# Graph network on one core: 15 of 416 edge blocks gathered by TensorE, and the edge stage joined with the segment sum

## The reference, cut to what matters

```python
h = relu(layernorm(x))                              # x after the first layer
e = concat([h[src], edge_attr], axis=1)             # 212500 x 128
e = e @ W1a + b1a                                   # 212500 x 128
e = relu(batch_norm(e, g1a, be1a))                  # mean and variance over all edges
# (e @ W2a + b2a is pulled behind the sum: W2a and W1b are multiplied once)
s = segment_sum(e, dst, 12500)                      # 12500 x 128
out = x + mlp(concat([h, s @ W2a + degree * b2a]))  # second batch norm, W1b, W2b
```

## Time and profile before

| | us |
|---|---|
| median of the runs shown | 5270.26 |
| profiled execution | 5270.57, its span 5268.7 |
| stages 1 to 3, to the first gather of stage 4 | 2513.8 |
| stage 4, first gather to the last block's statistics | 2086.0 |
| hand-over to the first running sum | 22.9 |
| stage 5, first running sum to the last | 533.6 |
| rest | 112.5 |
| GpSimd busy over the span | 3541.3 (67%) |
| VectorE busy over the span | 2374.1 (45%) |
| TensorE busy over the span | 2219.0 (42%), mean granted clock 0.659 |

### The profile page before, as it was taken

How to read it: one execution, slowest core, us unless ns; L and a number is a source line. 1 busy time by engine, 2 the same in 40 slices (tenths; PEclk the granted TensorE clock), 3 DMA queues, 4 the chain that set the end, 5 groups by cost and what they waited for, 6 DMA issues and landing times. The chain is left out here.

```text
span 5268.7 us, 27205 instructions
## 1 busy us (share of the span) xinstructions
PE 2219.0 (42%) x6378; PEld 1160.9 (22%) x6378; DVE 2374.1 (45%) x2946; ACT 1143.4 (22%) x1953; POOL 3541.3 (67%) x3749
## 2 busy tenths in 40 slices
PE   2012332323323232232454455455555555467766
PEld 2001111111111111110222222222222222255545
DVE  6224454544545444457222222222222222389995
ACT  8000000000000000001222222222222222178783
POOL 6677777777777777777677777777777777611112
PEclk7556666666666666665667666666666666678897
DMA  9723333333333333332333333333333333399993
GB/s 345 241 66 80 89 82 87 89 81 89 82 88 88 82 89 81 88 84 57 96 104 105 110 99 110 105 104 110 98 110 104 105 110 98 97 384 420 414 418 100
DMA packets 351656, 710.02 MB, mean 135 GB/s; under 512 B 146453, under 2 KB 218107, under 8 KB 304804
## 3 DMA queue, kind: packets, MB, share of 16 engines
q1 hardware_dynamic: 206258, 573.15, 31.6%
q0 software_dynamic: 119072, 128.58, 11.9%
q10 hardware_dynamic: 26166, 6.56, 0.6%
HBM read 363.45 MB, written 344.48 MB: 134 GB/s over the span
## 5 line engine op out<-in xcount | busy, mean ns | idle before, releaser
L1084 POOL DMA_INDIRECT pairs<-norm_table,node_sums x1664 | 1570.2, 944 | 520.1 <-issue 504.4
L836 POOL DMA_INDIRECT hid<-send_table,node_sums x1664 | 1570.3, 944 | 507.0 <-issue 507.0
L872 PE MATMUL ps_msg<-hidden,w_quarters 128*128 128x512 f32 x832 | 616.5, 909 | 1468.6 <-ACT hidden L901 1468.6
L1188 DVE TENSOR_SCALAR hid<-ps_hid,vec 128x512 f32<-128x512 f32 x416 | 312.2, 751 | 1463.1 <-PE ps_hid L1104 1462.8
L1097 PE MATMUL ps_pairs<-ident,pairs 128*128 128x128 f32 x1664 | 398.9, 386 | 1006.0 <-DMA pairs<-norm_table,node_sums 1005.4
L1104 PE MATMUL ps_hid<-pairs_t,w1a 128*128 128x512 f32 x832 | 701.1, 941 | 0.0
L872 PEld LDWEIGHTS ps_msg<-hidden,w_quarters 128*128 128x128 f32 x832 | 238.0, 301 | 1846.9 <-ACT hidden L901 1534.4
L940 DVE STREAM_TRANSPOSE send_t<-hid 128x1024 f32<-128x1024 f32 x104 | 131.0, 1260 | 1045.2 <-DMA hid<-send_table,node_sums 1045.2
L1097 PEld LDWEIGHTS ps_pairs<-ident,pairs 128*128 128x128 f32 x1664 | 265.7, 195 | 1449.8 <-issue 1282.0
L1136 ACT COPY pairs_t<-ps_pairs 128x512 f32<-128x512 f32 x416 | 243.6, 586 | 1485.9 <-PE ps_pairs L1097 1479.8
L901 ACT ACTIVATE hidden<-joined 128x1024 f32<-128x1024 f32 x104 | 109.9, 1056 | 1969.1 <-DVE joined L944 1969.1
(11 more groups left out here) (195 smaller groups left out, 1899.2 us busy)
## 6 DMA issues: line engine op xcount, KB each, us to landing
hid_edges<-hid SPq DMA_DIRECT2D x104, 1024.0 KB
hid<-hid_edges SPq DMA_DIRECT2D x104, 1024.0 KB, 10.9
hid_edges<-rows SPq DMA_DIRECT2D x104, 1024.0 KB
recv_edges<-node_sums SPq DMA_DIRECT2D x52, 1024.0 KB
hid<-recv_edges SPq DMA_DIRECT2D x416, 128.0 KB, 3.3
recv_edges<-hid SPq DMA_DIRECT2D x416, 128.0 KB, 2.3
edge_in<-in_edge_attr_dram SPq DMA_DIRECT2D x415, 128.0 KB, 4.6
hid<-send_table,node_sums POOLq DMA_INDIRECT x1664
```

Of the source, the lines that this page charges most:

```text
L836: pool.indirect_dma_start(out=send_in[:, s, j * C:(j + 1) * C], out_offset=None, in_=send_table, in_offset=bass.IndirectOffsetOnAxis(ap=sr ...
L872: mm = nc.tensor.matmul(ps_msg[k % M][:, d, :], w2_quarters[:, b, d, :], hidden[:, s % 2, b, :], start=b == 0, stop=b == BANDS - 1)
L1084: pool.indirect_dma_start(out=pairs[:, s, j, 0:C], out_offset=None, in_=norm_table, in_offset=bass.IndirectOffsetOnAxis(ap=src_cols[:, k / ...
L1188: nc.vector.tensor_scalar(part, ps_hid[s % 2][:, :], vec[:, 0:1], None, ALU.add).then_inc(hid_made, 1)
```

## The change

Five things change, all in stages 4 and 5.

1. **Products for gathers.** From block 36 on (`FIRST`), every 24 blocks form a group, 15 groups in all, and the last block of each has no indirect DMA. Its rows come from TensorE. In blocks 8 to 35 the table in SBUF is split into three bf16 parts (high, middle, rest) by ScalarE and VectorE. For the product block VectorE makes a small one-hot of "node number modulo 128" times "tile number + 1" (`make_own`), TensorE turns it into PSUM (`turn_own`), and over the 23 other blocks of the group VectorE makes 98 one-hot tiles of 128 x 512 bf16 out of it (`make_hot`, 8 buffers), four or five per block. For each of them TensorE runs two products (`add_tiles`): 128 columns for high and middle, 64 for the rest. ScalarE copies the sums out in three pieces, and `product` adds one more product with W1a's node half stacked twice.
2. **Last to first.** Blocks are walked from 415 down to 0, so that chunks 4 to 0 come last. They stay in SBUF, in a ring of five slots, and are neither stored nor loaded.
3. **One block of code.** Stages 4 and 5 have no barrier between them. The first relu waits for `affine_made` alone; the masks are loaded by SP in front of that.
4. **Statistics in parts.** Every 51 blocks VectorE aggregates their statistics into two sets of six; the last aggregation reads 16 sets instead of 416.
5. **Smaller moves.** Edge attributes are loaded straight into `pairs`, in pieces of 256 bytes, without ScalarE's copy. The running sum works in place, in the chunk's own slot, so that a slot is loaded again only when its chunk has been turned back.

The diff, cut to its core:

```diff
+            HR = 5
+            SPLIT = 3
+            TILES = NI
+            FIRST = U + 2 * NSTEP3
+            GROUP = 24
+            NPE = 15
+            OH = 8
+            hot_of = ps_mask[1][:, BLK:BLK + BLK // 2].bitcast(BF16)
...
+            def block_of(k):
+                return NBLK - 1 - k
+            def slot_of(c):
+                return c if c < HR else c % 2
+            def by_products(k):
+                g, at = group_of(k)
+                return 0 <= g < NPE and at == GROUP - 1
+            def tiles_of(k):
+                g, at = group_of(k)
+                if not 0 <= g < NPE or at == GROUP - 1:
+                    return range(0)
+                return range(TILES * at // (GROUP - 1), TILES * (at + 1) // (GROUP - 1))
...
-                def load(r, s):
-                    k = r * U + s
-                    at_least(sp, edge_copied, k - U + 1)
+                def load_pairs(r, s):
+                    k = r * U + s
+                    at_least(sp, turned, k - U + 1)
...
+                        sp.dma_start(pairs[:, s, :, C:2 * C], attr_v[block_of(k)]).then_inc(loaded[s], 16)
+                def store_hid(r, s):
+                    k = r * U + s
+                    c = chunk_of(k)
+                    if k % PER != PER - 1 or c < HR:
+                        return
...
+                sp.wait_ge(hot_used, TILES * NPE)
+                sp.dma_start(masks, same_sum.rearrange("(p c) -> p c", c=CO)).then_inc(masks_in, 16)
+                def load_hid(k, _):
+                    if k < HR:
+                        return
+                    at_least(sp, back_turned, 2 * (k - HR + 1))
+                    at_least(sp, sum_done, 2 * (k - HR + 1) + 1)
+                    sp.dma_start(hid[:, k % HR, :], hid_v[:, k, :]).then_inc(hid_back[k % HR], 16)
...
                 def gather(r, s):
                     k = r * U + s
-                    at_least_apart(pool, turned, k - U + 1, pool_passed)
+                    b = block_of(k)
+                    if by_products(k):
+                        return
+                    at_least(pool, turned, k - U + 1)
...
+                    own = by_products(k)
+                    if own:
+                        nc.tensor.matmul(ps_hid[s % 2], w_twice[:, :], sums_hm, start=True, stop=False)
+                    nc.tensor.matmul(ps_hid[s % 2], w1a[:, :], pairs_t[:, s % 2, :], start=not own, stop=True).then_inc(multiplied, 1)
...
+                def add_tiles(r, s):
+                    k = r * U + s
+                    g, _ = group_of(k)
+                    n = hot_count(k)
+                    for t in tiles_of(k):
+                        if t == 0:
+                            at_least(pe, last_made, NSTEP3)
+                            at_least(pe, sums_taken, 2 * g)
+                        at_least(pe, hot_made, n + 1)
+                        first, last = t == 0, t == TILES - 1
+                        nc.tensor.matmul(acc_hm, table_hm[:, t, :, :].rearrange("p h c -> p (h c)"), one_hot[:, n % OH, :], start=first, stop=last)
+                        mm = nc.tensor.matmul(acc_lo, table_lo[:, t, :], one_hot[:, n % OH, :], start=first, stop=last)
+                        mm.then_inc(hot_used, 1)
+                        n += 1
...
-                pipeline(pe, NBLK, U, [(0, turn), (1, product), (NODE_EVERY, product_node), (0, turn_node)])
+                pipeline(pe, NBLK, U, [(0, turn), (1, product), (2, product_node), (0, turn_node), (0, add_tiles), (0, turn_own)])
...
+                def make_hot(r, s):
+                    k = r * U + s
+                    g, _ = group_of(k)
+                    n = hot_count(k)
+                    for t in tiles_of(k):
+                        if t == 0:
+                            at_least(dve, own_turned, g + 1)
+                        at_least(dve, hot_used, n - OH + 1)
+                        nc.vector.tensor_scalar(one_hot[:, n % OH, :], hot_of, float(t + 1), None, ALU.is_equal).then_inc(hot_made, 1)
+                        n += 1
...
-                pipeline(dve, NBLK, U, [(0, finish)])
+                pipeline(dve, NBLK, U, [(0, split), (0, make_hot), (0, make_own), (3, finish), (3, aggregate)])
                 dve.wait_ge(stats_made, NBLK)
-                affine_of_norm(Chain(dve, sem("affine4")), root_ready, root_made, stats[:, :, :].rearrange("p k q -> p (k q)"),
+                affine_of_norm(Chain(dve, sem("affine4")), root_ready, root_made, parts[:, :, :].rearrange("p k q -> p (k q)"),
...
-        end_phase()
...
-        with ExitStack() as s5:
-            U = 12
-            R = 3
-            HR = 4
...
-                        at_least(act, loaded[s % HR], 16 * (r * (U // HR) + s // HR + 1))
+                    if h == 0 and k >= HR:
+                        at_least(act, hid_back[k % HR], 16 * (k // HR))
...
-                pipeline(sp, CHUNKS, U, [(5, store), (0, load), (8, confirm)])
+                pipeline(sp, CHUNKS, 1, [(0, load_hid), (4, store_rows), (7, confirm)])
```

More of the change, by code:

```diff
@@ new lines, in gnn_kernel @@
+            w_in, turned, copied, multiplied, hid_made, stats_made, root_ready, root_made, affine_made = (
+                sem(n + "4") for n in ("w_in", "turned", "copied", "multiplied", "hid_made", "stats_made", "root_ready", "root_made", "affine_made"))
+            hid_back = [sem(f"hid_back{i}") for i in range(HR)]
+            rows_out = [sem(f"rows_out{i}") for i in range(R)]
+            numbered, own_made, own_turned, hot_used, hot_made, sums_taken, high_made, rest_made, mid_made, last_made = (
+                sem(n + "4") for n in ("numbered", "own_made", "own_turned", "hot_used", "hot_made", "sums_taken", "high_made", "rest_made",
+                                       "mid_made", "last_made"))
@@ L1086, in gather @@
                                                 ).then_inc(gathered[s], 16)
                 pipeline(pool, NBLK, U, [(0, gather)])
+                pool.wait_ge(node_taken, NI_PAD)
+                pool.wait_ge(hot_used, TILES * NPE)
+                pool.wait_ge(chunks_out, HR)
+                for i in range(NI):
+                    needed = pool.value_load(chunks_needed[0:1, i:i + 1], min_val=1, max_val=CHUNKS)
+                    pool.wait_ge(chunks_out, needed)
+                    pool.sem_inc(pool_passed, 1)
+                    pool.indirect_dma_start(out=sum_in[:, i, :], out_offset=None, in_=sum_edges,
+                                            in_offset=bass.IndirectOffsetOnAxis(ap=end_idx[:, i:i + 1], axis=0)).then_inc(sums_got, 16)
@@ L1093, in turn @@
                     k = r * U + s
-                    at_least(pe, edge_copied, k + 1)
-                    at_least(pe, gathered[s], 16 * J * (r + 1))
+                    at_least(pe, loaded[s], 16 * (r + 1))
+                    at_least(pe, gathered[s], 16 * J * gathers_of(k))
                     for j in range(J):
@@ new lines, in _, with spread @@
+                pe.wait_ge(hid_made, NBLK)
+                pe.wait_ge(node_copied, NI_PAD)
+                pe.wait_ge(node_made, NI)
+                pe.wait_ge(sums_taken, 2 * NPE)
+                def spread(k, h):
+                    at_least(pe, sum_done, 2 * k - 1 + h)
+                    one_row = row_of[0:NCO, k:k + 1].broadcast_to([NCO, P])
+                    for a in range(0, HALF, BLK):
+                        mm = nc.tensor.matmul(ps_mask[h][:, a:a + BLK], one_row, masks[:, h * HALF + a:h * HALF + a + BLK], start=True, stop=True)
+                    mm.then_inc(mask_spread, 1)
@@ new lines, in turn_back @@
+                def turn_back(k, h):
+                    if h == 0:
+                        at_least(pe, sum_done, 2 * (k + 1))
+                    at_least(pe, rows_made, 2 * k + h - 1)
+                    for j in range(JS // 2):
+                        mm = nc.tensor.transpose(ps_back[h][:, j * P:(j + 1) * P], hid[:, k % HR, h * (JS // 2) + j::JS], ident[:, :])
+                    mm.then_inc(back_turned, 1)
+                pe.wait_ge(begun, 2)
+                pe.wait_ge(masks_in, 16)
@@ new lines, in copy_rows @@
+                def copy_rows(k, h):
+                    at_least(act, back_turned, 2 * k + h + 1)
+                    if h == 0:
+                        at_least(act, rows_out[k % R], 16 * (k // R))
+                    nc.scalar.copy(rows[:, k % R, h * HALF:(h + 1) * HALF], ps_back[h][:, :]).then_inc(rows_made, 1)
+                pipeline(act, CHUNKS, 1, [(0, lambda k, _: relu(k, 0)), (2, lambda k, _: copy_rows(k, 0)),
+                                          (0, lambda k, _: relu(k, 1)), (2, lambda k, _: copy_rows(k, 1))])
@@ L1326, in gnn_kernel @@
+                    part = hid[:, k % HR, h * HALF:(h + 1) * HALF]
+                    nc.vector.tensor_tensor_scan(part, ps_mask[h][:, :], part, before, ALU.mult, ALU.add).then_inc(sum_done, 1)
+                pipeline(dve, CHUNKS, 1, [(0, lambda k, _: running_sum(k, 0)), (0, lambda k, _: running_sum(k, 1))])
```

373 lines of the change are left out of this document (219 added, 154 removed).

## The result

The changed kernel takes 5174.95 us (median of four runs, 5173.9 to 5176.39). The kernel before, beside it, took 5270.03 (5268.15 to 5272.83): a ratio of 0.982, with a 95% interval of 0.9805 to 0.9834. 5166 was forecast, with a range of 5140 to 5230. The profiled spans are 5268.7 and 5173.8, 94.9 us apart.

| stretch | before | after | difference | forecast |
|---|---|---|---|---|
| to the first gather of stage 4 | 2513.7 | 2512.9 | -0.8 | 0 |
| first to last gather | 2076.1 | 2001.4 | -74.7 | -74.9 |
| last gather to last statistics | 10.0 | 8.2 | -1.8 | 0 |
| last statistics to first running sum | 22.87 | 3.38 | -19.5 | -19.6 |
| first running sum to the last one's end | 533.6 | 533.7 | +0.1 | -10.2 |

A forecast was written before the change was run, and what follows sets the result against it. GpSimd's issuing of gathers was taken to bound stage 4, and DMA transfers stage 5. Savings of 74.9 (gathers), 19.6 (hand-over) and 10.2 (stage 5), together 104.7, from 5270.57 gave 5166 us, range 5140 to 5230.

The forecast's parts named there:

- GpSimd sets the pace, 74.9 us: Stage 4: GpSimd, issuing gathers, is the engine waited for; 15 blocks x 4 gathers x 1.248 us leave the time.
- The others hold the new pace: Stage 4: per group VectorE (67 to 111 us) and TensorE (if its clock rises) fit into GpSimd's 114.9 us.
- the rivals' mechanism: Stage 4: groups outlast GpSimd's 114.9 us, through seams and long one-hots (5191 us, chance 0.17) or slow clock (5503, 0.10).
- The clock rises when TensorE has products between its waits: Stage 4 groups: TensorE waits less than before, reaching the mean clock of 0.71 to 0.89 it needs, against 0.65.
- The rule that was weighed as a rival: Stage 4: each wait slows TensorE, clock stays 0.65, groups 10 to 35 us longer, 5316 to 5690 us; chance 0.10.
- The hand-over, 19.6 us: Last statistics to first running sum: 3.3 us in place of 22.87, with short aggregation and no load in front.
- Stage 5, 10.2 us: Running-sum stage: five chunks needn't be loaded, so 523.4 us in place of 533.6; bounds of the saving 0 and 24.
- 7.4 + 525 - 8.6 = 523.4: Stage 5 length: transfers start 7.4 us after first running sum, take 525 at 418 GB/s; last sum ends 8.6 before last transfer.
- The other 24 us belong to the loads: Stage 5 before the change: 208 running sums need 510 us of 534; the remainder was put down to waiting for loads.
- The rival of 510 us: Stage 5 runs at VectorE's pace, 510 us in place of 523, if loads are freed; total 5152 us, chance 0.07.

## Why the prediction was right, and where it was not

**GpSimd sets the pace, 74.9 us: right.** 74.7 in the trace, 75.0 by taking the products out alone, and 9.05 more for two further blocks.

**The others hold the new pace: right, with less to spare on TensorE than on VectorE.** The one-hot was taken at 0.49 us and is 0.418; VectorE has 72 us per group, near the lower end of its 67 to 111. The Trainium skill, "VectorE: DVE Perf Modes", section "Why PSUM operands drop a tier", has two 16-bit elements per cycle from PSUM at most. The trace agrees, with 0.418 us against the f32 row's 0.751 and the 0.39 estimated from the page. TensorE went the other way. A pair of products was bounded by 0.40 and 0.61 us at the fast level, and starts lie 0.66 apart. A group came to 104.3 us of TensorE, the upper end of 83 to 104, at a clock of 0.96 where 0.71 to 0.89 was asked for. The high clock paid for the long pairs. The groups of 16 show what stood behind this step: where TensorE falls late, the time does come out of the total, and the rivals' mechanism is real (shown there by more work per group, not by a slower clock or longer one-hots). In the groups of 24 it was some 10 us away (114.9 - 104.3).

**The clock rises when TensorE has products between its waits: right.** 0.64 in the blocks of stage 4 ahead of the groups, 0.96 in them. Only 126 waits for gathers are left of 381. The rule that was weighed as a rival is that of the Trainium skill, "TensorE: Matmul & The Clock Gate", section "HAM oscillation — how this bites in real kernels", which tells of a kernel where every wait for a tile put the array back to its slow level. Here it is seen at single waits, as in the block above with its 1.09, but not at each: of the 83 waits for a gather in the groups, 29 are followed by transposes that take over 0.9 us, and the others, up to 3.12 us long, are not. The earlier trace rows had a block at the fast level behind a wait already (1.49 us), which the prediction read as agreeing with that rule.

**The hand-over, 19.6 us: right.** 19.5, by the steps named: 3.38 us where 3.3 was worked out. Of its parts, the chunks that stay were taken back by a run (8.1 us); the aggregation's 11.42 to 0.59 and the missing barrier are read from the traces alone.

**Stage 5, 10.2 us: wrong, it gave nothing.** The step that failed is "7.4 + 525 - 8.6 = 523.4". Each of its parts was off, and the prediction's 7.4 left out a step: SyncE asks for a chunk behind the store of the chunk that stood in the slot:

```profile
4535.89 0.34 SPq L1195 DMA_DIRECT2D hid_edges<-shared  x1
4536.32 0.37 SPq L1187 DMA_DIRECT2D ring<-hid_edges  x1
```

The first load goes out 10.4 us behind the first running sum (4525.91 to 4536.32), not 7.4. The transfers take 532.7 us to the gather that waits for the last store, at 5069.04, not 525. Most of the difference is at the ends: when no load is left, only stores run, and the last two windows above move 313 and 247 GB/s in place of 417, 2.6 MB or 6 us short. And that gather starts 9.4 us behind the last running sum, not 8.6. 10.4 + 532.7 - 9.4 is the measured 533.7. Said in bytes: stage 5 moved 412 x 533.58 = 219.8 MB before and 406 x 533.7 = 216.7 MB after, only 3.1 MB less in place of the 5.2 of five chunks, because the kernel before had brought in two of its chunks, 2.2 MB, during the hand-over; and the new start of 10.4 us without any transfer is worth more than those 3.1 MB at 417 GB/s, 7.4 us.

That the term was read as a matter of loads alone was a second error. "The other 24 us belong to the loads" is refuted: the run with half of the stores has no load waits and 530.65 us. The trace of the kernel before had shown it; VectorE's waits in the middle of its stage 5 are:

```profile
DVE total L1321 <- PE ps_mask L1271: 20.8, 50, 0.9
...
DVE total L1321 <- ACT hid L1294: 3.0, 11, 0.3
```

The 24 was itself too large: the 9.80 us of the earlier trace rows are three steps from start to start and one last duration of 2.35, so a step is 2.48 us, and VectorE's pace for the stage is 516 us, not 510. Two limits stand there at almost the same length, the DMA engines (533.65 with TensorE's order mended) and TensorE's order (530.65 with the bytes taken away). Only without both does the stage come to VectorE's pace (517.65). Had the transfers come out as the prediction had them, TensorE would still have held the gain at about 3 us, as the run with half of the stores shows. The rival of 510 us failed for the same reason.

The total missed by 9 us. The missing 10 us of stage 5 are nearly all of it; -0.8, -1.8 and +1.7 elsewhere, which were not forecast, cancel to -0.9. The 1.7 us of the rest were not explained.

## What to carry to other kernels

A sum over the bytes of a stage is worth a forecast only with its ends: what came in before the stage began, when the first transfer is asked for in the queue's own order, and what runs when one direction has no work left. Where a stage is longer than its busiest engine, look for every wait of about the same length, since taking one away shows the next; two edits that each gave 0 to 3 us gave 16 together. And moving work to an idle engine pays one for one as long as that engine's time per period, read from start to start and not from its shortest durations, stays under the period of the engine that is relieved.

## What the runs showed of the hardware

In stage 5 the busy share of the DMA engines did not follow the rate in proportion. It is 0.99 at 406 GB/s in the changed kernel, and 0.88 at 314 GB/s with half of the stores, where nothing waits for a load: the share fell by 11% and the rate by 23%. And the clock of TensorE in the groups was higher than the working dared to ask for: 0.96 with fifteen products and 0.99 with seventeen, in a loop that had 0.64 ahead of the groups and still stops for gathers. The pairs of bf16 products started 0.66 us apart at the fast level, where a pair by itself had taken 0.61.
